# 32-expert selection: ranks by scaled-identity matmuls and ScalarE, one-hots of four tiles at once

## The reference

```python
x = x + relu(grouped_conv3x3(layer_norm(x)) + bias)           # 8 groups
t = t + moe32(layer_norm(t))                                  # 32 experts
x = x + window_attention(layer_norm(x))                       # 8x8 windows, 16 heads
t = t + moe8(layer_norm(t))                                   # 8 experts, top 2 of each token
```

```python
Sm = softmax(xf @ W_router + b_router)            # 4096 x 32
G_ek, idx_ek = top_k(Sm.T, k)                     # k = 4096 // 32 = 128 tokens for each expert
act = silu(tokens @ W_up[group] + b_up)           # tokens = xf[idx_ek]; 4 experts share one W_up
Eout = act @ W_down[e] + b_down[e]
y = zeros.at[idx_ek].add(G_ek[..., None] * Eout)
```

## Time and profile before

| | us |
|---|---|
| median of 3 timed runs | 682.73 |
| all three | 682.73, 683.02, 677.84 |
| the profiled execution | 677.05 |
| its span on the core | 675.2 |
| mean granted clock of PE, share of full | 0.831 |

### The profile page before, as it was taken

How to read it: one execution, slowest core, us unless ns; L and a number is a source line. 1 busy time by engine, 2 the same in 40 slices (tenths; PEclk the granted TensorE clock), 3 DMA queues, 4 the chain that set the end, 5 groups by cost and what they waited for, 6 DMA issues and landing times.

```text
span 675.2 us, 14949 instructions
## 1 busy us (share of the span) xinstructions
PE 476.4 (71%) x4930; PEld 372.7 (55%) x4930; DVE 413.6 (61%) x1166; ACT 370.5 (55%) x789; POOL 329.6 (49%) x339
## 2 busy tenths in 40 slices
PE   4998511136557654158999999745799999899944
PEld 1355400112345443136778787414799888898944
DVE  4586688898211112389999999989244434344456
ACT  2488376427121212128787876520688777687833
POOL 3000000000688787276888888211727777777540
PEclk9999555559687778558999999975699999899987
DMA  7012469100264643610000000345201111111128
GB/s 276 2 35 63 98 196 346 66 0 0 61 156 103 158 104 31 206 56 2 2 4 2 3 3 3 95 105 150 90 18 52 51 55 54 52 52 52 38 79 326
DMA packets 40328, 54.79 MB, mean 81 GB/s; under 512 B 10240, under 2 KB 30784, under 8 KB 39872
## 3 DMA queue, kind: packets, MB, share of 16 engines
q1 hardware_dynamic: 29584, 40.51, 19.0%
q0 software_dynamic: 10240, 13.12, 8.7%
q10 hardware_dynamic: 432, 0.23, 0.1%
HBM read 34.40 MB, written 19.43 MB: 80 GB/s over the span
## 4 chain that ended last, share of the span: by engine, by line
POOL 31%; issue 20%; PE 19%; DVE 13%; ACT 8%; DMA 7%; SPq 1%; DVEq 0%; POOLq 0%; ACTq 0%
POOL results L616 8%; POOL arena L585 7%; PE psum L1515 4%; POOL arena L607 4%; PE psum L1487 3%; POOL scratch L531 3%; ACT arena_b L1309 3%; POOL v_x L575 2%; DMA arena<-normed,gather_i 2%; PE psum L1804 2%; POOL x_tok L568 2%; PE psum L1810 2%; POOL y_odd L540 2%; POOL x_tok L592 2%; ACT arena_b L1307 2%
## 5 line engine op out<-in xcount | busy, mean ns | idle before, releaser
L531 POOL DMA_INDIRECT scratch<-table,idx x32 | 31.4, 980 | 172.0 <-DVE idx L878 162.6
L607 POOL DMA_INDIRECT arena<-normed,gather_i x64 | 61.9, 968 | 45.7 <-DVE gather_i L1140 25.1
L616 POOL DMA_INDIRECT results<-extra,dest_i x64 | 63.0, 985 | 37.9 <-DVE extra L1186 23.6
L1186 DVE SCALAR_TENSOR_TENSOR extra<-scratch,owned,extra 128x128 f32 x71 | 25.1, 353 | 84.5 <-issue 55.3
L585 POOL TENSOR_TENSOR arena<-arena,peak 128x1024 f32<-128x1024 f32 x32 | 60.9, 1902 | 25.5 <-DVE peak L990 25.5
L1428 ACT COPY arena_b<-w_sb 128x768 f32 x71 | 58.6, 825 | 20.2 <-issue 19.1
L1487 PE MATMUL psum<-cst,arena 128*128 128x128 f32 x320 | 54.2, 285 | 18.5 <-DMA arena<-normed,gather_i 15.1
L1804 PE MATMUL psum<-scratch,arena_b 128*128 x426 | 63.6, 287 | 0.1
L1810 PE MATMUL psum<-scratch,arena_b 128*128 x426 | 61.1, 281 | 0.0
L1820 PE MATMUL psum<-arena 128*128 128x128 f32 x426 | 59.4, 277 | 0.0
L1338 ACT ACTIVATE arena_b<-psum,bu_sb 128x512 f32<-128x512 f32 (+1 forms) x24 | 16.4, 685 | 77.8 <-PE psum L1630 77.8
(11 more groups left out here) (268 smaller groups left out, 1168.8 us busy)
## 6 DMA issues: line engine op xcount, KB each, us to landing
arena<-in_w_down_dram SPq DMA_DIRECT2D x8, 768.0 KB, 4.6
w_sb<-in_w_dram SPq DMA_DIRECT2D x3, 1536.0 KB, 11.1
table<-extra SPq DMA_DIRECT2D x8, 256.0 KB, 2.3
y_even<-x_tok SPq DMA_DIRECT2D x16, 128.0 KB
y_odd<-zeros SPq DMA_DIRECT2D x4, 512.0 KB
normed<-extra SPq DMA_DIRECT2D x8, 256.0 KB, 2.3
x_image<-x_tok SPq DMA_DIRECT2D x16, 128.0 KB
x_tok<-x_image SPq DMA_DIRECT2D x1, 2048.0 KB, 8.4
```

The lines of the kernel that those rows point to most:

```text
L531: nc.gpsimd.indirect_dma_start(out=rows_b[:, e // 4 % 4, e % 4, :], out_offset=None, in_=table[:, :], in_offset=bass.IndirectOffsetOnAxis( ...
L607: nc.gpsimd.indirect_dma_start(out=rows_d[:, t % ROWS_D, :], out_offset=None, in_=normed[:, :], in_offset=bass.IndirectOffsetOnAxis(ap=gat ...
L616: nc.gpsimd.indirect_dma_start(out=results[:, :], out_offset=bass.IndirectOffsetOnAxis(ap=dest_i[:, t:t + 1], axis=0), in_=y_ring[:, t % R ...
```

## The change

- Ranks. The marks become f16. PE computes one column at a time: two after the first count, the third (ties) after the second. ACT turns the running sums into `place` (f16): an offset is added to the sum of those above, and for ties a Relu of the limit minus the sum. DVE makes `tie_won`, the ties within the limit, in two halves. The transposition and the sum are one: PE adds 32 f16 matmuls of 128 columns (`turn`, eight blocks of four sources: marks, place of those above, ties won, place of ties) to two f16 matmuls of 512 columns that hold the shift. The moving operand is the identity times 1, -1 or 4096.
- Digits. ACT makes `hi16` from PSUM, DVE `lo16`. The low digit is one higher and so is the table `slot_lo`.
- One-hots. DVE compares four tiles in one instruction (1024 and 2048 elements), with two buffers of four tiles, in `scratch`; ACT makes its four products one after the other; the loops are unrolled. The token products were ACT's before too.
- POOL prepares the constants `ones16`, `shift16` and `turn16` after its first two memsets.
- The semaphores of the x loads serve the first four of `f_back` too; the counts waited for change with them.

The core of the diff:

```diff
 SEG = TOKENS // 4
@@ -104,7 +106,7 @@
...
+        n_above, n_tied = (scratch[:, SEG * k:SEG * (k + 1)] for k in (2, 3))
+        place, _ = shared(scratch, SEG * 4, [P, 2, SEG], F16)
+        shift16 = sb("shift16", [P, 1], F16)
+        place_base = sb("place_base", [P, 2])
+        tie_limit = sb("tie_limit", [P, 1])
...
+        oh_lo, at = shared(scratch, at, [P, 2, 4, 16, EXPERTS_B], F16)
         picked = sb("picked", [P, 2, 16, 16])
         ids_f = sb("ids_f", [P, 2, 16])
             nc.gpsimd.memset(zeros[:], 0.0).then_inc(s_zero, 1)
+            nc.gpsimd.memset(ones16[:], 1.0)
+            nc.gpsimd.memset(shift16[:], (PLACE_SHIFT - CHOSEN_SHIFT) / P)
+            pool.wait_ge(ld_ident, 16)
+            for k, factor in enumerate((1.0, -1.0, float(CHOSEN_SHIFT))):
+                ins = nc.gpsimd.tensor_scalar(turn16[:, k, :], ident, factor, None, ALU.mult)
...
-            nc.vector.tensor_scalar(banks(above), psum[:, 0:2, :], thr[:].bitcast(F32), None, ALU.is_gt, ALU.add,
-            nc.vector.tensor_scalar(banks(tied), psum[:, 0:2, :], thr[:].bitcast(F32), None, ALU.is_equal, ALU.add,
-            nc.vector.tensor_tensor_scan(n_above, zeros[:], above, 0.0, ALU.add, ALU.add).then_inc(dve_seq, 1)
-            nc.vector.tensor_tensor_scan(n_tied, zeros[:], tied, 0.0, ALU.add, ALU.add).then_inc(dve_seq, 1)
-            nc.vector.tensor_copy(offs[:], psum[:, 3, 0:2]).then_inc(dve_seq, 1)
-            nc.vector.scalar_tensor_tensor(n_above, n_above, offs[:, 0:1], above, ALU.add, ALU.mult).then_inc(dve_seq, 1)
-            nc.vector.scalar_tensor_tensor(n_tied, n_tied, offs[:, 1:2], tied, ALU.add, ALU.mult).then_inc(dve_seq, 1)
-            nc.vector.scalar_tensor_tensor(n_above, n_above, PLACE_SHIFT - 1.0, n_tied, ALU.add, ALU.add).then_inc(b_pos, 1)
+            for k, op, ranks in ((0, ALU.is_gt, n_above), (1, ALU.is_equal, n_tied)):
+                nc.vector.tensor_scalar(banks(marks[:, k]), psum[:, 0:2, :], thr[:].bitcast(F32), None, op, ALU.add,
+                                        accum_out=count[:, k:k + 1]).then_inc(b_tot, 1)
+                dve.wait_ge(b_tot, 2 * k + 1)
+                nc.vector.tensor_tensor_scan(ranks, zeros[:], marks[:, k], 0.0, ALU.add, ALU.add).then_inc(b_tot, 1)
+            dve.wait_ge(act_seq, 3)
+            dve.wait_ge(b_tot, 4)
+            for a in range(2):
+                half = slice(HALF * a, HALF * (a + 1))
+                nc.vector.scalar_tensor_tensor(tie_won[:, half], n_tied[:, half], tie_limit[:, 0:1], marks[:, 1, half],
+                                               ALU.is_le, ALU.mult).then_inc(b_pos, 1)
...
             for a in range(2):
-                dve.wait_ge(b_ptr, a + 1)
-                nc.vector.tensor_scalar(hi_v[:, a], psum[:, a, :], 1 / 16, -7.5 / 16, ALU.mult, ALU.add).then_inc(dve_seq, 1)
-                dve.wait_ge(dve_seq, dve_n.next())
+                dve.wait_ge(b_hi, a + 1)
                 nc.vector.scalar_tensor_tensor(lo_v[:, a], hi_v[:, a], -16.0, psum[:, a, :], ALU.mult,
                                                ALU.add).then_inc(dve_seq, 1)
                 dve_n.next()
             dve.wait_ge(dve_seq, dve_n.now())
-            with dve.Fori(0, TILES // 4) as i:
-                for k in range(4):
-                    u, b = 4 * i + k, k
-                    dve.wait_ge(b_ohmm, u + 1)
-                    nc.vector.tensor_tensor(oh_hi[:, b], hi16[:, bass.ds(u, 1), :].rearrange("p o (h e) -> p (o h) e", h=2)
...
-                    nc.vector.tensor_tensor(oh_lo[:, b], lo16[:, bass.ds(u, 1), :].to_broadcast([P, 16, EXPERTS_B]),
-                                            slot_lo[:], ALU.is_equal).then_inc(b_oh, 1)
-            dve.wait_ge(b_ohmm, 4 + TILES)
+            def onehots(n):
+                b, tiles = n % 2, slice(4 * n, 4 * n + 4)
+                if n > 1:
+                    dve.wait_ge(b_ohmm, 4 * (n - 1))
+                nc.vector.tensor_tensor(oh_hi[:, b].rearrange("p k h a e -> p (k h) a e"),
+                                        hi16[:, tiles, :].rearrange("p k (h e) -> p (k h) e", h=2).unsqueeze(2)
+                                        .to_broadcast([P, 8, 8, 16]),
+                                        slot_hi[:, 0:1].to_broadcast([P, 8, 8, 16]), ALU.is_equal).then_inc(b_ohhi, 1)
+                nc.vector.tensor_tensor(oh_lo[:, b], lo16[:, tiles, :].unsqueeze(2).to_broadcast([P, 4, 16, EXPERTS_B]),
+                                        slot_lo[:].unsqueeze(1).to_broadcast([P, 4, 16, EXPERTS_B]),
+                                        ALU.is_equal).then_inc(b_oh, 1)
+
+            for n in range(BLOCKS):
+                onehots(n)
+            dve.wait_ge(b_ohmm, TILES)
...
+            act.wait_ge(b_off, 1)
+            nc.scalar.activation(place_base[:, 0:1], psum[:, 3, 0:1], ACT.Copy, bias=float(CAP)).then_inc(act_seq, 1)
+            act.wait_ge(act_seq, 1)
+            nc.scalar.activation(place_base[:, 1:2], psum[:, 3, 1:2], ACT.Identity, scale=-1.0,
+                                 bias=place_base[:, 0:1]).then_inc(act_seq, 1)
+            act.wait_ge(act_seq, 2)
+            act.wait_ge(b_tot, 2)
+            nc.scalar.activation(place[:, 0], n_above, ACT.Identity, bias=place_base[:, 1:2]).then_inc(b_place, 1)
+            act.wait_ge(b_off, 2)
+            nc.scalar.activation(tie_limit[:], psum[:, 2, 4:5], ACT.Copy, scale=-1.0, bias=float(CAP)).then_inc(act_seq, 1)
+            act.wait_ge(act_seq, 3)
+            act.wait_ge(b_tot, 4)
+            for a in range(2):
+                half = slice(HALF * a, HALF * (a + 1))
+                nc.scalar.activation(place[:, 1, half], n_tied[:, half], ACT.Relu, scale=-1.0,
+                                     bias=tie_limit[:, 0:1]).then_inc(b_place, 1)
+            for a in range(2):
+                act.wait_ge(b_ptr, a + 1)
+                nc.scalar.activation(hi_v[:, a], psum[:, a, :], ACT.Copy, scale=1 / 16, bias=-8.5 / 16).then_inc(b_hi, 1)
+
+            token0 = const_at["token_id"][0]
+            for n in range(BLOCKS):
+                b = n % 2
+                act.wait_ge(b_ohhi, n + 1)
+                if n > 1:
...
-                    u, b = 4 * i + k, k
-                    act.wait_ge(b_ohhi, u + 1)
-                    act.wait_ge(b_ohmm, u + 1)
-                    nc.scalar.activation(oh_id[:, b].rearrange("p h a e -> p (h a e)"),
-                                         oh_hi[:, b].rearrange("p h a e -> p (h a e)"), ACT.Copy,
-                                         scale=cst[:, bass.ds(token0 + u, 1)]).then_inc(b_ohid, 1)
+                    at = token0 + 4 * n + k
+                    nc.scalar.activation(oh_id[:, b, k].rearrange("p h a e -> p (h a e)"),
+                                         oh_hi[:, b, k].rearrange("p h a e -> p (h a e)"), ACT.Copy,
+                                         scale=cst[:, at:at + 1]).then_inc(b_ohid, 1)
...
-            pe.wait_ge(b_tot, 2)
-            nc.tensor.matmul(psum[:, 3, 0:2], C("earlier_segment"), count[:, 0:2], start=True, stop=False,
-                             skip_group_check=True)
-            nc.tensor.matmul(psum[:, 3, 1:2], C("same_expert"), count[:, 0:1], start=False, stop=True,
-                             skip_group_check=True).then_inc(b_off, 1)
-            pe.wait_ge(b_pos, 1)
+            def one_column(at, parts):
+                for n, (matrix, col) in enumerate(parts):
+                    ins = nc.tensor.matmul(at, C(matrix), count[:, col:col + 1], start=n == 0, stop=n == len(parts) - 1,
+                                           skip_group_check=True)
+                return ins
...
+            pe.wait_ge(b_tot, 1)
+            one_column(psum[:, 3, 0:1], [("earlier_segment", 0)])
+            one_column(psum[:, 3, 1:2], [("same_expert", 0)]).then_inc(b_off, 1)
+            pe.wait_ge(b_tot, 3)
+            one_column(psum[:, 2, 4:5], [("earlier_segment", 1), ("same_expert", 0)]).then_inc(b_off, 1)
+            pe.wait_ge(s_zero, 2)
+
+            def turn(g, source, factor, **flags):
+                return nc.tensor.matmul(psum[:, g // 4, P * (g % 4):P * (g % 4 + 1)], source[:, P * g:P * (g + 1)],
+                                        turn16[:, factor, :], start=False, skip_group_check=True, **flags)
+
+            for a in range(2):
+                nc.tensor.matmul(psum[:, a, :], ones16[:], shift16[:, 0:1].to_broadcast([P, 512]), start=True, stop=False,
+                                 skip_group_check=True)
             for g in range(8):
-                ins = transpose(psum[:, g // 4, P * (g % 4):P * (g % 4 + 1)], n_above[:, P * g:P * (g + 1)])
-                if g % 4 == 3:
-                    ins.then_inc(b_ptr, 1)
-            pe.sem_inc(b_ohmm, 4)
+                turn(g, marks[:, 0], 2, stop=False)
+            pe.wait_ge(b_place, 1)
+            for g in range(8):
+                turn(g, place[:, 0], 0, stop=False)
+            for a in range(2):
+                pe.wait_ge(b_pos, a + 1)
```

(13 more changed lines are left out.)

42 lines of the change are left out of this document (18 added, 24 removed).

## The result

The changed kernel's median is 678.28 us (20 runs; 19 of them from 671.72 to 681.07, and one, disturbed, at 750.91), against 680.35 for the kernel before on the same chip (20 runs, 676.39 to 684.33): a ratio of 0.9941, 95% interval 0.9914 to 0.9969 (without the disturbed run). That is 0.6% faster, within the 1% that the prediction called no change, and 0.3 us from its 678. The ratio follows the averages, 680.4 and 676.5, which differ by 3.8 us; the two medians differ by only 2.1, since the runs of the changed kernel lie in two groups, seven at 671.7 to 674.0 and twelve at 676.3 to 681.1, and the median falls into the slower one. The profiled execution took 671.72 (span 669.9), 5.3 less than that of before [677.05, span 675.2].

A forecast was written before the change was run, and what follows sets the result against it. No single engine bounds the kernel; the stretch from threshold to first gather lies wholly on its chain of waits. Saving 1.7 + 2.7 - 0.4 = 4.0 us from 682.7 gives 678.7, stated as 678, range 672 to 682.5.

The forecast's parts named there:

- Ranks: From the first threshold comparison to the first one-hot: 13.4 us instead of 15.14, 1.7 us saved.
- the spacing of the 128-column matmul: PE's 32 turns in the ranks: 0.16 us each, 5.1 in all; 0.107 would save 3.4, 0.22 nothing.
- One-hots: From the first one-hot to the picking of the ids: 15.8 us instead of 18.46, 2.7 us saved.
- The start: GpSimd's new constants beside VectorE's first norm, near 6 to 7.5 us: 0.4 us lost, bounds 0 and 1.4.
- Picking to gather: From the picking of the ids to the first indirect DMA: unchanged at 4.16 us.
- The sum: Whole kernel: 1.7 + 2.7 - 0.4 = 4.0 us less.
- Rival 1: PE bounds the ranks (0.22 a matmul) or ScalarE the one-hots (0.508 a product): 680.5 to 682 us; chance 0.22.
- The sign that the prediction named for this rival: In the one-hot blocks: ScalarE shows no idle.
- Rival 2: PE's clock comes up earlier, during turns and blocks: 5 us saved, 677.7; its chance lies within the main case's 0.65.
- its objection: Against an earlier clock: PE's pause of about 1.4 us between the last turn and the first one-hot.
- Rival 3: The wide one-hot comparisons lose the packed rate: 3.34 us a block, 8.8 us slower, 691; chance 0.04.
- Rival 4: GpSimd's chain behind the stretch absorbs the gain, nothing changes at the end: 682.7 us; chance 0.09.

The follow-up runs named there:

- a0: The changed kernel again, unedited, as a reference beside its parts: median 674.19 us (4 runs), ratio 0.9883 to the kernel before.
- e_warm: The changed kernel with 17 unused matmuls of 384 columns in PE's pause ahead of the one-hots: median 675.17 us, ratio 0.9941 to the kernel before.
- e_late: The changed kernel with GpSimd's five constant instructions moved from 6 us to behind its other waits: median 676.49 us, ratio 0.989 to the kernel before.
- e_ranks: The changed kernel's new ranks with the old one-hot loops and buffers: median 678.31 us, ratio 0.993 to the kernel before.
- e_onehots: The old ranks (f32 arithmetic, eight f32 transposes) with the changed kernel's new one-hots: median 679.34 us, ratio 0.9946 to the kernel before.
- b0: The kernel before again, unedited, for a second trace: median 680.58 us, ratio 0.9987; its profiled execution took 683.92 us.
- e_full: The changed kernel with turns in earlier-free PSUM banks, late GpSimd constants, 15 unused matmuls ahead of the one-hots, 10 ahead of the ids: 672.29 us, ratio 0.9881.
- e_turns: The changed kernel with 16 more turns, the factor 4096 issued as twice 2048: median 677.62 us, ratio 0.9947 to the kernel before.
- e_conv: e_full with two unused f32 matmuls of 288 columns ahead of the second convolution group: median 673.59 us, ratio 0.9886 to the kernel before.
- e_prewarm: The changed kernel with twice 7 unused matmuls of 384 columns ahead of the first and third columns of counts: 675.51 us, ratio 0.9933.

## Why the prediction was right, and where it was off

*Ranks, forecast 1.7 saved, measured 3.6 (a0) and 4.2 (first comparison).* The mechanism held: f32 arithmetic gone, ScalarE's products hidden, PE's queue last. VectorE's starts came within 0.1 of the forecast once shifted by the later threshold (second scan 136.33, forecast 135.75 + 0.6; tie_won from 138.73, forecast 138.05 + 0.6). Relu brought no table load. The term that was mis-sized is the spacing of the 128-column matmul, taken as 0.16 from a row of strided loads, with bounds 0.107 and 0.22. It is 0.107 at 0.50: 32 turns in 3.62 instead of 5.1, 1.5 us; the turns also began 0.3 earlier behind the first comparison than forecast (6.54 in a0 for 6.81). In the first comparison the clock rose in mid-turns as well: the turns took 0.7 less, the stage 0.6. The forecast stood in the middle of its bounds, and the lower bound was measured. What failed is the reading of the f16 row of 64 columns. It took the row's 0.131 (0.125 from start to start, (4.20 − 0.31) / 31) as columns plus a load that stays exposed, and laid 64 more columns mostly on top. Behind 128 columns no load was exposed. Whether that is because the load has twice the columns to hide behind or because it is contiguous here and strided there, no run separated; the loads themselves lasted the same, 0.149 in that row (its median in the trace of before) and 0.151 in a0, which gives the layout no support.

*One-hots, forecast 15.8, measured 15.82 (first comparison) and 15.49 (a0).* The mechanism and its prices were met: 0.69 and 1.22 an instruction, 1.74 to 1.75 a block, products 0.42 apart, and steps of 2.06 in the first blocks at half clock, which e_warm took away. That the sum agrees to 0.02 is luck: the seven steps took 12.84 for 12.66 forecast, and the end behind them 2.98 for 3.15. The 0.33 between the two profiles is one step of 2.06 more or less.

*The start, forecast 0.4 lost, measured 0.19* (e_late).

*Picking to gather, forecast unchanged, measured 0.15 to 0.4 less* in the changed kernel, none in e_ranks and e_onehots (4.16): the four f32 matmuls of the ids take 0.62 with the clock still up and up to 1.04 with it down (e_warm).

*The sum.* By stages 7.0 − 0.2 = 6.8 us were saved, for 4.0 forecast. Yet the ratio 0.9941 is 4.0 us (2.1 to 5.9), and the spans of the two profiles differ by 5.3. The whole span in parts, in us; the last column has the shortest and the longest of all thirteen profiles:

| | before | b0 | changed | all thirteen |
|---|---|---|---|---|
| start to gate_bits | 82.2 | 84.9 | 82.8 | 82.2 to 85.4 |
| to the first gather (the edited stretch is in here) | 86.4 | 86.5 | 79.5 | |
| experts, to the attention's first add | 127.2 | 129.5 | 127.2 | 126.3 to 131.5 |
| attention | 126.8 | 128.2 | 128.1 | 126.8 to 128.5 |
| to dest_i | 47.9 | 49.1 | 49.0 | 47.3 to 49.1 |
| to the end | 204.7 | 203.9 | 203.3 | 202.8 to 205.8 |

The 6.9 won up to the gather met 0.6 lost at the start, 1.3 in the attention and 1.1 up to dest_i, and 1.4 won behind it: 5.3. Executions of one kernel differ as much in each of these parts (before and b0 in the first three, the changed kernel and a0, with 205.1, in the last), so none of them can be put down to the change. For the 1.1 there is a sight in the windows, a dip of the clock to 0.50 at 420 to 430 in the changed kernel's profile where that of before has 1.00. Changed kernel, then before:

```profile
420.00:430.00 10.00, 9.32 (x82) 6.77 (x82) 7.99 (x34) 4.37 (x7) 2.46 (x5) 0.50 0.19 55
```

```profile
420.00:430.00 10.00, 6.97 (x137) 5.98 (x136) 9.63 (x27) 7.05 (x11) 6.22 (x9) 1.00 0.03 9
```

The ten profiles with such a dip take 48.9 to 49.1 for that part, the three without (before, e_onehots, e_full) 47.3 to 47.9. b0 has it, so it comes without the change too. But nine of the ten profiles with the new ranks have it and one of the three with the old, too few to say whether the change makes it more frequent.

Each timed run lists its mean granted clock, and in the first comparison time goes with it: seven runs of the changed kernel at 0.826 to 0.836 took 671.7 to 674.0, twelve at 0.815 to 0.823 took 676.3 to 681.1 (correlation −0.89; over the 28 runs of before beside e_turns, −0.74). That speaks for the clock as a source of the spread, but doesn't show it: which stage was slow in a run without a profile isn't seen, and the part that varies most between the profiles, the experts with 5.2 us, has a mean clock of 0.69 to 0.72 in all of them.

So the agreement of 678 with 678.28 is luck. The forecast started from 682.73, a median of three runs that lies 2.4 above the 680.35 of twenty. From there it took off 4.7 us, the 4.0 of the sum and 0.7 for a median that might fall lower, where the two medians differ by 2.1; the two errors cancel. The 4.0 itself met an average difference of 3.8, while the stages won 6.8, which is outside the interval of this comparison. The measurement of a0, with 0.9883 (8.0 us, 5.1 to 10.9), has it inside. Where the rest of the 6.8 went in the first comparison stays open.

*The rivals.* Rival 1 was true of its first half in mechanism (PE does bound the ranks) and wrong in price, 0.107 for 0.22; in the one-hots ScalarE did not bind: no engine waited for one of its products in these profiles, and VectorE kept its 1.74. But it is close. Of its 2.5 us idle 2.3 are the start (1.59) and two waits behind late blocks (0.37 each); at full clock it has no gap, 24 products in 10.39 us in a0, 1.73 a block. The sign that the prediction named for this rival, no idle of ScalarE, thus came without the rival. Rival 2 came true in one profile (clock at 1.00 from 140) and for 0.7 us, and its objection held too: the pause took the clock away again. Rival 3 is refuted: 0.69 and 1.22, the packed lengths, with three free dimensions. Rival 4 is refuted: the gather started as much earlier as the stretch was shorter, a later threshold aside, the experts' part behind it took the same 127.2, and the interval of the ratio excludes no gain.

## What to carry to other kernels

Where a block of work moves to PE as many small matmuls, price the spacing from both ends, and don't add a load to the columns that can cover it: with 128 columns and a contiguous stationary operand the columns alone were the price here. Once one engine's queue is shortened, count what stands behind the next engine's last result before expecting more: moving 10 matmuls out of the way gained 0.24 us, since 16 stood behind VectorE in either order. A change of 1% can be read in the stages of one trace, while the totals of a dozen runs tell it to about 2 us. The stretch as a whole came out as 30.79 and 30.80 in two profiles, its parts moved by 0.6 with the clock; so compare sums, and look at the clock before reading a part. And don't forecast an absolute time from three runs: the base was off by more than half of the saving.

## What the runs showed of the hardware

- The granted clock dipped in steady PE work: to 0.72 to 0.75 at 18 to 24 us in seven of the thirteen profiles (gate_bits from 84.1 on, against 82.2 to 83.5 in the others; PE busy for 5.9 to 6.0 of the 6 us), and to 0.50 to 0.72 over ten microseconds between 410 and 440 in ten, the kernel before among them (b0). What sets them off is open; e_conv was to tell and did not.
- Spare matmuls in a pause of PE change what follows: with 3.7 us of them right behind the turns the clock was at 1.00 for all the one-hots (e_warm, e_full), where a0 had 0.50 for the first blocks; while two groups of 2.40 us ran, with the counts between them, it stayed at 0.50 (e_prewarm).
- f16 loads of 128 contiguous columns were hidden fully behind 128-column matmuls at 1.2 GHz (0.107 a pair).
- GpSimd's tensor_scalar of 128x128 from f32 to f16 took 0.53 (three in 1.64), longer than the 0.46 of its add, and cost VectorE's four norms beside them 0.19 in all. The Trainium skill, "SBUF — State Buffer", section "Who interferes with whom", has VectorE in a two-port mode and GpSimd shut each other out for whole instructions; the trace agrees that they interfere, and the loss was less than one of GpSimd's instructions.
